# Aggregating one span of columns at a time, deferring the last part of the layer-2 product, spreading the bias adds and splitting the token statistics in a GNN and MoE kernel

## The reference, cut to what matters

```python
def gcn_conv(x, W, b, src, dst, n):
    h = x @ W.T
    ...
    norm = dinv[s] * dinv[d]
    msg = h[s] * norm[:, None]
    out = jax.ops.segment_sum(msg, d, num_segments=n)
    return out + b
...
h = relu(gcn_conv(layernorm(x), W1, b1, src, dst, n))   # 512 -> 128
z = gcn_conv(h, W2, b2, src, dst, n)                     # 128 -> 64
y = relu(z @ Wd1.T + bd1)                                # 64 -> 128
y = relu(y @ Wd2.T + bd2)                                # 128 -> 256
x = x + y @ Wd3.T + bd3                                  # 256 -> 512
...
t = layernorm(x)                                         # the tokens
for e in range(8):                                       # each token has 2 of 8 experts
    h = gelu(t[tokens of e] @ w1[e])                     # 512 -> 256
    out[tokens of e] += weight * (h @ w2[e])             # 256 -> 512
```

## Time and profile before

| | |
|---|---|
| median of 3 runs | 191.72 us (191.26 to 191.94) |
| profiled execution, its own time | 192.37 us |
| its span in the trace | 190.6 us |
| TensorE busy | 165.4 us (87%) |
| VectorE busy | 130.9 us (69%) |
| ScalarE busy | 93.0 us (49%) |
| GpSimd busy | 96.2 us (50%) |
| matmuls of the aggregations (line 1531) | 150 records, 29.1 us |

### The profile page before, as it was taken

The page is one execution under the profiler, slowest core; times in us unless marked ns, Lnnn a source line. Parts: engine busy times, 40 slices in busy tenths (PEclk is TensorE's granted clock), DMA queues, the critical chain, the costliest instruction groups (busy, mean ns, idle before and its releaser), DMA issues.

```text
span 190.6 us, 3626 instructions
## 1 busy us (share of the span) xinstructions
PE 165.4 (87%) x1179; PEld 115.6 (61%) x1179; DVE 130.9 (69%) x304; ACT 93.0 (49%) x202; POOL 96.2 (50%) x74
## 2 busy tenths in 40 slices
PE   4599799999997999479999999779999999999900
PEld 1288578887884665166554454249877777687500
DVE  2898999999995999937031859562697669664210
ACT  3437677777877530034045127021986777644310
POOL 5099999999990000000007000686008888763662
PEclk9999999999999999979999999985999999999995
DMA  4994000000004899980000005247915366543564
GB/s 123 299 331 126 2 2 3 3 0 3 3 0 88 274 380 367 365 293 10 0 0 3 0 0 220 69 132 252 379 54 70 79 127 82 101 48 51 72 80 64
DMA packets 15547, 21.71 MB, mean 114 GB/s; under 512 B 3135, under 2 KB 8001, under 8 KB 15525
## 3 DMA queue, kind: packets, MB, share of 16 engines
q1 hardware_dynamic: 12994, 16.02, 25.6%
q0 software_dynamic: 2432, 5.24, 15.7%
q10 hardware_dynamic: 98, 0.17, 0.2%
HBM read 15.19 MB, written 6.23 MB: 112 GB/s over the span
## 4 chain that ended last, share of the span: by engine, by line
PE 57%; DVE 15%; POOL 9%; DMA 6%; issue 6%; ACT 4%; POOLq 1%; ACTq 0%; DVEq 0%
PE bank L1428 9%; PE bank L1670 8%; PE bank L1531 7%; PE bank L1697 5%; PE bank L1403 4%; PE bank L1641 4%; PE bank L1681 4%; PE bank L1700 3%; DVE x_sb L896 3%; DVE ring L705 3%; PE bank L1682 3%; DMA out<-at,to_i 3%; POOL first_viol L598 2%; POOL out L647 2%; DMA x_rows<-at 2%
## 5 line engine op out<-in xcount | busy, mean ns | idle before, releaser
L616 POOL TENSOR_SCALAR_AFFINE_SELECT before<-ones_bf 128x128 bf16<-128x128 bf16 x1 | 37.8, 37836 | 0.0
L647 POOL DMA_INDIRECT out<-at,to_i x16 | 23.9, 1494 | 20.9 <-DVE at L1063 10.1
L1428 PE MATMUL bank<-ring 128*128 128x110 bf16 x324 | 29.9, 228 | 5.2 <-DVE ring L705 3.7
L1531 PE MATMUL bank<-at,ring 128*128 128x512 bf16 (+1 forms) x150 | 29.1, 353 | 0.5 <-ACT ring L1197 0.5
L1428 PEld LDWEIGHTS bank<-ring 128*128 128x128 bf16 x324 | 20.5, 101 | 12.0 <-issue 5.1
L705 DVE TENSOR_TENSOR ring<-iota_slots,lo 128x1024 bf16<-128x1024 f16 (+1 forms) x41 | 27.4, 667 | 0.0
L1156 ACT CAST at<-bank 128x400 f32 (+1 forms) x41 | 20.6, 503 | 10.9 <-PE bank L1434 8.7
L705 DVE TENSOR_TENSOR ring<-iota_dst,key 128x880 bf16<-128x880 f16 (+1 forms) x41 | 24.3, 594 | 0.0
L1531 PEld LDWEIGHTS bank<-at,ring 128*128 128x128 bf16 x150 | 14.9, 101 | 13.2 <-issue 1.1
L1670 PE MATMUL bank<-at_r 128*128 128x512 f32 (+1 forms) x64 | 21.8, 404 | 0.0
L1003 DVE TENSOR_TENSOR ew_r<-ew,at_r 128x1024 fp32r<-128x1024 f32 x16 | 19.3, 1216 | 0.0
(11 more groups left out here) (208 smaller groups left out, 297.0 us busy)
## 6 DMA issues: line engine op xcount, KB each, us to landing
ew<-in_w SPq DMA_DIRECT2D x16, 512.0 KB, 9.6
x_sb<-in_x SPq DMA_DIRECT2D x9, 256.0 KB, 5.4
out<-x_sb SPq DMA_DIRECT2D x9, 256.0 KB
wd3t_sb<-in_Wd3T SPq DMA_DIRECT2D x1, 512.0 KB, 4.9
x_rows<-xn SPq DMA_DIRECT2D x1, 512.0 KB, 2.8
x_rows<-at SPq DMA_DIRECT2D x1, 512.0 KB, 3.5
w1t_sb<-in_W1T SPq DMA_DIRECT2D x1, 256.0 KB, 4.9
bd_sb<-in_bd SPq DMA_DIRECT2D x1, 256.0 KB, 4.3
```

What stands on the lines that cost most here:

```text
L616: nc.gpsimd.affine_select(out=before[:, :], in_=ones_bf[:, :], compare_op=ALU.is_gt, fill=0.0, base=0, pattern=[[1, P]], channel_multiplie ...
L647: nc.gpsimd.indirect_dma_start(out, bass.IndirectOffsetOnAxis(to_i[0:n, i, e:e + 1].bitcast(mybir.dt.uint32), 0), y_out[0:n, e % 2, i], No ...
L1428: last = mm(to, hot_src[:, j, t], hot_dst[:, j, t], start=(t == 0 and not ends), stop=(first and t == tiles - 1), skip_group_check=not ends)
L1531: last = mm(bank[4 + i][:, 0:n], parts[k][:, s], at[:, s, a:a + n], start=(k == 0 and s == 0), stop=(k == last_k and s == CH - 1))
```

## The change

1. **By span.** In both aggregations part 0 still goes source by source. Then each span gets all its other parts before the next span begins. `rank_assignments` moves ahead, right behind `spread_dinv`. `product_h2(0)` stands after part 1 of span 1, `product_h2(1)` after part 2 of span 2.
2. **Eight sources.** The second aggregation starts with the sources of chunks 0 to 7; `product_h2(2)`, which makes the last two, is issued ahead of chunk 8. Its parts `part2` and `part3` move from `ring` into a free piece of `xnt`, since `ring` is still read.
3. **The bias.** The ten adds of `bd3` leave their place ahead of the routing: eight go between the slot tables and the scaling of the second aggregation, two behind it. The `gate` goes into the dense path.
4. **Decoder.** `decode3(0)` to `decode3(3)` go first, then `decode1(2)`, `decode2(1)`, `decode2(2)` (in banks 2 and 3 now), then `decode3(4)` to `decode3(8)`; `decode3(9)` goes behind `transpose_gathered(0)`.
5. **Statistics in halves.** After chunk 1 and again after chunk 3 of the tokens: root, reciprocal, normalised rows. ScalarE normalises chunks 0 and 1, VectorE chunks 2 and 3. ScalarE loads the table of Gelu right after `finish_y2(2)`.
6. **Results.** `y_out` has three buffers, and VectorE's `keep_results(e - 1)` comes ahead of the wait for `s_hs_hi`. `weights_rest(1)` moves up to after chunk 7.

```diff
-            dve.wait_ge(s_wg, 16 * NWG)
-            for c in range(CH):
-                last = v.tensor_tensor(x_sb[:, c], x_sb[:, c], bd3_sb[:, :], ALU.add)
-            link(last)
...
+            add_bias(0, CH - 2)
             for i, (a, n) in enumerate(SPANS):
                 dve.wait_ge(s_agg2, i + 1)
                 v.tensor_tensor(zt[:, a:a + n], bank[4 + i][:, 0:n], dinv_row[:, a:a + n], ALU.mult).then_inc(s_agg2s, 1)
+            add_bias(CH - 2, CH)
...
-                    if c == TC - 1:
+                    if c % 2:
+                        i, a = c // 2, c - 1
                         ins.then_inc(s_mv2, 1)
-                        dve.wait_ge(s_mv2, 1)
-                        dve.wait_ge(s_std2, 1)
+                        dve.wait_ge(s_mv2, i + 1)
+                        dve.wait_ge(s_std2, i + 1)
...
-                    if e >= 2:
-                        dve.wait_ge(s_added[e % 2], 32 * (e // 2))
+                    if e >= KEPT:
+                        dve.wait_ge(s_added[(e - KEPT) % 2], 32 * ((e - KEPT) // 2 + 1))
...
+                    if e >= 1:
+                        keep_results(e - 1)
                     dve.wait_ge(s_hs_hi, e + 1)
                     v.tensor_tensor(hs[:, e % 2, 1], hs_raw, hs[:, e % 2, 0].bitcast(F32), ALU.subtract).then_inc(s_hs_lo, 1)
-                    if e >= 1:
-                        keep_results(e - 1)
...
             finish_y1(1)
+            take_deviations(0)
+            act.wait_ge(s_rstd2, 1)
+            for c in range(2):
+                normalise_tokens(c)
             finish_y1(2)
+            take_deviations(1)
             finish_y2(1)
...
                 for i in range(len(SPANS)):
-                    for s in range(CH):
-                        wait_part(last_k, s)
-                        last = add(last_k, s, [i])
-                    last.then_inc(done, 1)
-                    after_span(i)
+                    for k in range(1, last_k + 1):
+                        for s in range(CH):
+                            wait_part(k, s)
+                            last = add(k, s, [i])
+                        if k == last_k:
+                            last.then_inc(done, 1)
+                        after_pass(i, k)
...
+            def last_product(s):
+                if s == CHUNKS[2][0]:
+                    product_h2(2)
...
-            neighbours([part2, part3], wait_part2, s_agg2, lambda i: decode1(0) if i == 1 else None)
+            neighbours([part2, part3], wait_part2, s_agg2, lambda i, k: decode1(0) if i == 1 else None, at_chunk=last_product)
             decode2(0)
             decode1(1)
-            for c in range(CH):
-                if c == TC - 1:
-                    decode2(1)
+            for c in range(TC):
                 decode3(c)
-                if c == 0:
-                    decode1(2)
-                if c == TC:
-                    decode2(2)
+            decode1(2)
+            decode2(1)
+            decode2(2)
+            for c in range(TC, CH - 1):
+                decode3(c)
...
-                pe.wait_ge(s_x2, CH)
                 transpose_gathered(0)
+                decode3(CH - 1)
                 transpose_gathered(1)
```

More of the change, by code:

```diff
@@ L892, in _ @@
             last.then_inc(s_value, 1)
-            dve.wait_ge(s_wg, 16 * NWG)
-            for c in range(CH):
-                last = v.tensor_tensor(x_sb[:, c], x_sb[:, c], bd3_sb[:, :], ALU.add)
-            link(last)
-            for c in range(TC):
-                for k in range(TOPK):
-                    last = v.tensor_scalar(gate_part[:, k, c], expert_no[:, :], gif[:, c, k:k + 1], gw_sb[:, c, k:k + 1],
-                                           ALU.is_equal, ALU.mult)
-            link(last)
-            link(v.tensor_tensor(gate[:, :, :], gate_part[:, 0], gate_part[:, 1], ALU.add))
             routed = [0]
@@ L1067, in _ @@
                 gathered_rest(0)
+                sum_rows(CH - 1)
                 gathered_rest(1)
@@ L1084, in _ @@
             with dve.If(dense != 0):
+                sum_rows(CH - 1)
+                for c in range(TC):
+                    for k in range(TOPK):
+                        last = v.tensor_scalar(gate_part[:, k, c], expert_no[:, :], gif[:, c, k:k + 1], gw_sb[:, c, k:k + 1],
+                                               ALU.is_equal, ALU.mult)
+                last.then_inc(s_gate, 1)
+                dve.wait_ge(s_gate, 1)
+                v.tensor_tensor(gate[:, :, :], gate_part[:, 0], gate_part[:, 1], ALU.add).then_inc(s_gate, 1)
+                dve.wait_ge(s_gate, 2)
                 for c in range(TC):
@@ L1263, in _, with take_deviations @@
             finish_y1(1)
+            def take_deviations(i):
+                act.wait_ge(s_mv2, i + 1)
+                nc.scalar.activation(rstd[:, 1, 2 * i:2 * i + 2], mv[:, 2 * i:2 * i + 2, 1], ACT.Sqrt,
+                                     bias=eps[:, :]).then_inc(s_std2, 1)
+            take_deviations(0)
+            act.wait_ge(s_rstd2, 1)
+            for c in range(2):
+                normalise_tokens(c)
             finish_y1(2)
+            take_deviations(1)
             finish_y2(1)
[L1267 to L1271 removed]
             finish_y2(2)
+            nc.scalar.activation(table_use[:, :], one[:, :], ACT.Gelu)
             with act.If(sparse != 0):
@@ L1551, in neighbours @@
-                if before_last:
-                    before_last()
-                for i in range(len(SPANS)):
-                    for s in range(CH):
-                        wait_part(last_k, s)
-                        last = add(last_k, s, [i])
-                    last.then_inc(done, 1)
-                    after_span(i)
+                for s in range(CH):
+                    if at_chunk:
+                        at_chunk(s)
+                    wait_part(0, s)
+                    add(0, s, range(len(SPANS)))
@@ new lines, in neighbours @@
+                with pe.If(slow != 0):
+                    for kk in range(len(parts)):
+                        wait_part(kk, CH - 1)
+                    with pe.Fori(0, CH) as s:
+                        for of in parts:
+                            for i, (a, n) in enumerate(SPANS):
+                                mm(bank[4 + i][:, 0:n], of.rearrange("p c n -> p (c n)")[:, bass.ds(s * P, P)],
+                                   at2[:, :, :].rearrange("p c n -> p (c n)")[:, bass.ds(s * NP + a, n)],
+                                   start=False, stop=False)
```

126 lines of the change are left out of this document (67 added, 59 removed).

## The result

The changed kernel took 194.25 us (median of four executions, 193.37 to 195.77), the kernel before 191.64 beside it (191.26 to 191.94): ratio 1.0145, 95% interval 1.0079 to 1.0212. The forecast was 185.7 and faster. The profiled execution has a span of 191.6 us against 190.6. The ratios leave out executions that lie more than 1.5% above a kernel's fastest (of `stores_up` that is seven of ten), the medians leave out none, and since the changed kernel turns out to have more than one time of its own, I go by the medians.

A forecast was written before the change was run, and what follows sets the result against it. Bounds: waits between engines, TensorE's half clock behind them, the decoder's way to the token store, serial index adds. Gains 0.5 + 1.9 + 2.4 + 1.2 = 6.0 us off the median 191.72 gave 185.7, range 184.1 to 188.8.

The forecast's parts named there:

- First aggregation: First product_h2 without TensorE's wait of 3.77 us, at 74.9 instead of 82.04; slot rows done at 82.3.
- The new stall: Inside the second aggregation, TensorE waits for the parts of product_h2(2), 87.3 to 88.9, 1.6 us.
- The bias takes it back: Eight bias adds on VectorE hold span 0's scaling until 95.6; decode1(0) at 97.1, gain 0.5 us, TensorE idle 2.6.
- First rival: Clock falls at TensorE's new wait ahead of decode1(0): costs 1.7 us (to 3.3), 187.4 us (to 189.0); chance 0.25.
- the main case: The whole kernel at 185.7 us, own range 184.9 to 186.6; chance 0.43.
- Statistics and gathers: Decoder to first gathers: token store at 113.0 (gain 2.5), gather 0 at 121.7, up(0) at 126.8 (gain 2.4).
- The clock: No gap at the gathers, so no clock fall; up(0) to down(0) in 5.76 us, gain 2.4, down(0) at 132.6.
- a wait of TensorE between experts: Listed sign in the expert part that would show the forecast wrong; given no size.
- The tail: At the end, the add at 174.90 and the later index adds with their landings come 1.2 us earlier.
- The bound 0: At the end, lower bound of the gain, 0 us, if the series of landings had another floor.
- The sum: Whole kernel: 0.5 + 1.9 + 2.4 + 1.2 = 6.0 us gained, giving 185.7 us.

The follow-up runs named there:

- stores_up: The change with the stores of x_sb held back until the up products of expert 1 are done: 193.03 us, the change beside it 193.42.
- C: The change with six of ten bias adds moved into VectorE's idle time ahead of scale_h2(2): 183.69 us, the change beside it 187.75.
- again4: The change itself, unchanged, measured on its fifth occasion: 193.42 us (189.94 to 194.65), the kernel before 192.91.
- E: The change with the token statistics back in one root of four chunks after chunk 3: 197.04 us, the change beside it 193.61.
- the undisturbed trace: The change itself, unchanged, measured a second time, without late increments: 187.75 us (span 185.8), the kernel before 192.32.
- D: The change with two result buffers and keep_results behind the wait for s_hs_hi again: 189.48 us, the change beside it 187.75.
- final: The change with product_h2(2) ahead of source 4, bias adds in idle time and expert 4's gathers held back: 183.45 us, before 191.91.

## Why the prediction was wrong

**First aggregation: right.** Product at 74.95 (forecast 74.9), no wait, second aggregation at 81.56 (82.3).

**The new stall: right.** 1.44 us (forecast 1.6), and TensorE on at 87.90 (88.9).

**The bias takes it back: right in kind.** Scaling at 94.78 (95.6), `decode1(0)` at 96.27 (97.1), wait 2.80 (2.6). The register loads are the 0.47 of "issue" ahead of the adds, the top of the range 0 to 0.5. Gain 1.3 instead of 0.5.

**First rival: it happened.** The clock fell behind that wait in every trace that has it, and C prices it at 1.77 (forecast 1.7). It had 0.25 and should have been the main case. The Trainium skill's rule (TensorE: Matmul & The Clock Gate, "HAM oscillation"), that waiting between bursts brings the lower clock, agrees at 96 us; at 134.6 in again4 the trace has a wait of 0.86 behind one of 1.23 and no fall, and in stores_up one of 0.80 and no fall.

**Statistics and gathers: right within 0.7.** Store 113.72 (113.0), gather 0 used at 122.08 (121.7), up(0) 127.26 (126.8), gain 1.9 instead of 2.4 with the half clock in it. That is so near partly by luck: from `decode1(0)` to up(0) it took 1.3 longer than forecast (30.99 for 29.7), but `decode1(0)` had come 0.8 early. I counted nothing for the halves on TensorE's side; E shows 1.6.

**The clock, the step that failed.** The forecast put down(0) at 132.6, 5.8 behind up(0), on the ground that no gap at the gathers means no fall, and took from the old trace that TensorE has no wait from the first up product on. In the undisturbed trace it is right: 5.89. On four of five occasions TensorE's increments came up to 2.6 us late, up(1) waited 1.4 to 2.15 us, and in three of the four traces 6.8 us at half clock followed: down(0) 136.55, down(1) 5.1 later than undisturbed. My text named "a wait of TensorE between experts" as what would show it wrong, but no rival priced one.

**The tail: mechanism there, size wrong.** The add for down(5) came 3.22 behind its start instead of 4.47, as forecast 1.2 earlier. It did not reach the end: the last add waited 2.49 for a landing in the first trace. From down(6) to the end: before 15.25, undisturbed 14.67, first trace 15.32. The bound 0 was the better one; D gives 0.3.

**The sum** against the undisturbed trace: 1.9 at up(0), 2.3 between up(0) and down(0), 0.6 at the end, 4.8 of 6.0 forecast (spans 190.6 and 185.8). That 187.75 is what the first rival said (187.4), not the main case. The result of the first occasion is that sum with 5.8 taken back: the 5.1 and the tail.

**What is shown and what is open.** Shown: the late increments, the wait, and what both cost. Shown on one disturbed occasion, by one kernel of five executions: they go when the gathers of expert 4 stay away from up(0) and up(1). They don't need the stores, which seem to lengthen them. Open: what disturbs an occasion. It is not the program and not the chip. Since increments are missing from the records of every disturbed trace, the recording of the profile may itself hold them up; every execution here has its span and clock from a profile, so no run can tell. That the trace of before has none of it says little, since its records are complete: its gathers (130.41 and 131.67) and stores (from 129.40) lie around up(0) in the same way, but no trace of it from a disturbed occasion was kept. Its time is 191.64 to 192.91 on disturbed and undisturbed occasions alike; there TensorE was at half clock at up(0), which may leave the handovers more slack, but it was not tried to slow TensorE down there.

## What to carry over

A wait that the change removes had slack behind it for others: once TensorE runs through at full clock, each handover between engines is on the path, and one late semaphore of 2 us costs 5. Where a program issues indirect DMAs in a burst, it may pay to hold those that aren't needed yet until the short handovers are over. Measure on several occasions before you believe a few per cent, count the records of two traces before you explain what differs between them, and compare traces from a mark behind the chance clock falls.

## What the runs showed of the hardware that I had not expected

- Increments of TensorE up to 2.6 us late, on four of five occasions with the same program, and in the first trace those of DMAs with them (8 instead of 64 between 129.24 and 132.00) while packets went on.
- VectorE's bias add takes 0.61 us alone and 1.4 beside GpSimd's casts, and four casts take 4.9 us instead of the 3.98 that they take alone, at 99.84 in the trace of before. In final:

```profile
92.47 0.68 DVE L956 TENSOR_TENSOR x_sb<-x_sb,bd_sb 128x512 f32<-128x512 f32 x1
...
93.91 4.90 POOL L632 CAST at_r<-ew 128x1024 fp32r<-128x1024 f32 x4 [36.11 <-PE bank L1561]
94.15 2.79 DVE L956 TENSOR_TENSOR x_sb<-x_sb,bd_sb 128x512 f32<-128x512 f32 x2
```

- The clock falls for 3.4 us near 60 us in 13 of 20 traces of kernels that are alike up to there; it costs some 1.5 us.
